# First aggregation of a two-layer graph network: sorted gathers against merged edge blocks scattered with add into four DRAM copies

## The reference

```python
h = relu(layernorm(x))
agg = zeros_like(h).at[src].add(edge_attr)          # first aggregation, key src
...                                                  # attention over one condition row
h = relu(concat([h, agg, x_with_cond], 1) @ W1.T + b1)
x = x + h @ W2.T + b2
h = relu(layernorm(x))
ht = relu(h @ V1 + c1)
msg = sigmoid(exp(wp) * ht[src] + bp)
fsum = segment_sum(msg, dst, 6250)                   # second aggregation, key dst
...                                                  # logit, a matmul, a row norm
```

## Time and profile before

| | us |
|---|---|
| median of three runs | 3203.99 |
| lowest, highest | 3202.18, 3206.39 |
| span of the profiled execution | 4012.8 |
| first aggregation within that span | 368 to 1985 |
| second aggregation within that span | 2201 to 3800 |

### The profile page before, as it was taken

One profiled execution on the slowest core, in us unless ns is written; L12 is line 12 of the kernel. 1 busy time (PEld: TensorE's weight loads), 2 busy tenths in 40 slices (PEclk: granted clock), 3 DMA queues, 4 the chain that ended last, 5 costly groups with the idle time before them and its releaser, 6 DMA issues. The chain is left out here.

```text
span 4012.8 us, 65381 instructions
## 1 busy us (share of the span) xinstructions
PE 2786.4 (69%) x12081; PEld 2045.6 (51%) x12081; DVE 2746.8 (68%) x6119; ACT 2007.6 (50%) x5317; POOL 1848.1 (46%) x1875
## 2 busy tenths in 40 slices
PE   1883777677767776777786677767776777777754
PEld 1552554455545555555575455545555555555543
DVE  7887777667777777677774577777776775444456
ACT  1343565455546554565325455555554655554434
POOL 0225455555554555455312555645555555555400
PEclk9996888888888888888898788888888888888787
DMA  3001222322232223222335222422232223322412
GB/s 105 0 0 46 70 69 71 73 70 69 70 76 68 71 69 79 68 70 65 72 134 169 76 69 72 75 67 69 70 72 74 71 71 69 81 81 81 70 39 77
DMA packets 129255, 287.68 MB, mean 72 GB/s; under 512 B 31200, under 2 KB 59798, under 8 KB 129174
## 3 DMA queue, kind: packets, MB, share of 16 engines
q0 software_dynamic: 84480, 230.80, 22.7%
q1 hardware_dynamic: 42918, 53.84, 4.2%
q10 hardware_dynamic: 1776, 2.23, 0.2%
HBM read 260.68 MB, written 26.06 MB: 71 GB/s over the span
## 5 line engine op out<-in xcount | busy, mean ns | idle before, releaser
L1088 PE MATMUL bank<-oh,ring 128*128 128x256 f32 x7040 | 2110.7, 439 | 351.3 <-DVE agg L888 259.8
L1088 PEld LDWEIGHTS bank<-oh,ring 128*128 128x128 f32 x7040 | 1428.9, 221 | 667.0 <-issue 337.0
L888 DVE TENSOR_TENSOR agg<-bank,agg 128x512 f32 x1760 | 1208.4, 687 | 783.8 <-remote 353.1
L426 POOL DMA_INDIRECT ring<-in_edge_attr,idxst x880 | 877.0, 997 | 766.8 <-DVE idxst L869 501.9
L426 POOL DMA_INDIRECT ring<-g_table,idxst x880 | 850.7, 967 | 735.8 <-DVE idxst L869 457.1
L831 DVE SCALAR_TENSOR_TENSOR ohr<-iota,cst 125x256 f16<-125x256 f16 x1600 | 763.7, 479 | 222.6 <-issue 76.9
L549 ACT ACTIVATE oh<-dist 128x256 f32<-128x256 f32 x1760 | 648.9, 407 | 532.7 <-PE bank L1088 255.9
L536 ACT ACTIVATE dist<-iota,nlst 128x256 f32<-128x256 f32 x1760 | 746.6, 494 | 15.0 <-ACT nlst L530 1.8
L1088 PE MATMUL bank<-mov,ohr 125*128 125x220 f16 x1920 | 379.9, 285 | 457.1 <-DVE mov L639 397.6
L542 ACT ACTIVATE smov<-iota,scst 125x220 f16<-125x220 f16 x560 | 236.7, 469 | 798.8 <-PE bank L1088 422.7
L1088 PEld LDWEIGHTS bank<-mov,ohr 125*128 125x128 f16 x1920 | 170.1, 104 | 654.4 <-DVE mov L639 498.9
(11 more groups left out here) (180 smaller groups left out, 1669.4 us busy)
## 6 DMA issues: line engine op xcount, KB each, us to landing
ring<-in_edge_attr,idxst POOLq DMA_INDIRECT x880
ring<-g_table,idxst POOLq DMA_INDIRECT x880
x_scratch<-ring SPq DMA_DIRECT2D x25, 256.0 KB, 2.0
ring<-x_scratch SPq DMA_DIRECT2D x25, 256.0 KB, 3.4
y_scratch<-ring SPq DMA_DIRECT2D x25, 256.0 KB, 2.4
g_table<-ring SPq DMA_DIRECT2D x25, 256.0 KB, 2.2
pre<-y_scratch SPq DMA_DIRECT2D x25, 256.0 KB, 2.6
agg<-in_x SPq DMA_DIRECT2D x4, 1536.0 KB
```

Of the source, the lines that this page charges most:

```text
L426: gp.indirect_dma_start(out=ring_rows[:, b, j, :], out_offset=None, in_=table, in_offset=bass.IndirectOffsetOnAxis(ap=idxst[:, t:t + 1], a ...
L888: dve.tensor_tensor(to, pt[j][:, :], to, ALU.add).then_inc(s_acc, 1)
L1088: return pe.matmul(o, l, r, start=start, stop=stop, skip_group_check=skip)
```

## The change

The first aggregation has no sort any more (SORTS = 4, all for the second one). The edges are taken in input order.

- SP streams `edge_attr` in 196 blocks of 512 edges (EBLKS, 512 KB each) into four slots that lie in `agg`; partition p holds edges 4p to 4p+3 of the block.
- The keys `src` come once more as floats, transposed by PE in the prologue into `scol`: a column for every tile of 128 edges (ETILES = 784).
- For a tile PE broadcasts the 128 keys along the columns of a PSUM bank (`key_rows`), DVE compares them with the keys on the partitions (`find_same`), masks the result by a triangle and counts it. PE multiplies this 128x128 matrix by the edge rows (`sum_rows`), so that one row of each set of equal keys holds the sum. `first_rows` and `targets` turn the count into an index: the node's row where this is that row, otherwise one of 128 rows behind the nodes ("trash").
- ACT copies the sums from PSUM (two tiles at a time) into eight slots `merged`.
- POOL issues one indirect DMA for each tile, which scatters 128 rows of 1 KB with add into one of four copies of the aggregate in DRAM, tile t into copy t mod 4. Before it POOL waits for the tile that went into the same copy before.
- The four copies, 6400 rows of 1 KB each, are filled with zeros at the start by four DMAs on ACT's queue, behind the weights. Their source is the first tenth of `pre`, so `pre_out` waits for them.
- rank 1 is dealt out over the first 58 blocks, a step a block, on DVE and PE.
- The pass over the windows first adds the copies up: ACT issues four loads of 256 KB for each window into one of two buffers (in `msk` and `cum`), POOL adds them (three adds of 128x512), PE transposes, ACT copies into `agg`; then the pass goes on as before. x is loaded from the end of the front stage on.

The code for the new stage and for this pass is written out without loops.

```diff
-SORTS = 2 * GROUPS
+SORTS = GROUPS
+EB = 4
+EBLK = EB * P
+EBLKS = -(-E // EBLK)
+ETILES = EB * EBLKS
+COPIES = 4
+AROWS = NBLK * P
+ESLOTS = 4
+MSLOTS = 8
+QSLOTS = 3
...
@@ SP
-            sp.wait_ge(s_mm, BODY + GROUPS * TILES)
+            sp.wait_ge(s_h, NW)
+            for b in range(EBLKS):
+                if b >= ESLOTS:
+                    sp.wait_ge(s_m1, 2 * (b - ESLOTS) + 2)
+                rows = P if b + 1 < EBLKS else ELAST
+                sp.dma_start(edge_ring[0:rows, b % ESLOTS, :, :],
+                             a["edge_attr"][b * EBLK:b * EBLK + rows * EB, :].rearrange("(p j) f -> p j f", j=EB)
+                             ).then_inc(s_el[b % ESLOTS], 16)
+
+            sp.wait_ge(s_pv, 2 + NW)
...
@@ POOL
-            gp.wait_ge(s_h, NW)
-            gp.memset(agg[:, :], 0.0).then_inc(s_z, 1)
-            gp.wait_ge(s_a1, 2 + NW)
+            gp.wait_ge(s_zf, 16 * COPIES)
+            for t in range(ETILES):
+                b, j, r = t // EB, t % EB, t % COPIES
+                if j == 0:
+                    gp.wait_ge(s_ix, b + 1)
+                if j % 2 == 0:
+                    gp.wait_ge(s_mg, t // 2 + 1)
+                if t >= COPIES:
+                    gp.wait_ge(s_sa[r], 16 * (t // COPIES))
+                gp.indirect_dma_start(out=aggc_dram[r][:, :], out_offset=bass.IndirectOffsetOnAxis(ap=idx1[:, b, j:j + 1], axis=0),
+                                      in_=merged[:, t // 2 % MSLOTS, (t % 2) * D:(t % 2 + 1) * D], in_offset=None,
+                                      compute_op=ALU.add).then_inc(s_sa[r], 16)
+
+            for n in range(NW):
+                c0, c1, c2, c3 = fold[n % 2]
+                gp.wait_ge(s_fc[n % 2], 16 * COPIES * (n // 2 + 1))
+                gp.tensor_tensor(c0, c0, c1, ALU.add).then_inc(s_fa, 1)
+                gp.tensor_tensor(c2, c2, c3, ALU.add).then_inc(s_fa, 1)
+                gp.wait_ge(s_fa, 3 * n + 2)
+                gp.tensor_tensor(c0, c0, c2, ALU.add).then_inc(s_fa, 1)
...
-            gathers(a["edge_attr"], 0)
...
@@ ACT
+            act.wait_ge(s_zt, 1)
+            for r in range(COPIES):
+                act.dma_start(aggc_dram[r].rearrange("(p c e) f -> p c (e f)", p=P, c=5),
+                              zeros.unsqueeze(1).to_broadcast([P, 5, 10 * D])).then_inc(s_zf, 16)
+
...
                 hold(act, s_a1, n + 3)
+                hold(act, s_zf, 16 * COPIES)
...
-            with act.Fori(0, GROUPS) as g:
-                onehots(g, True)
...
+            for h in range(2 * EBLKS):
+                act.wait_ge(s_m1, h + 1)
+                if h >= MSLOTS:
+                    for t in (2 * (h - MSLOTS), 2 * (h - MSLOTS) + 1):
+                        act.wait_ge(s_sa[t % COPIES], 16 * (t // COPIES + 1))
+                act.copy(merged[:, h % MSLOTS, :], pt[h % 4][:, :]).then_inc(s_mg, 1)
...
+            def fold_load(n):
+                if n >= 2:
+                    act.wait_ge(s_ft, n - 1)
+                for r in range(COPIES):
+                    act.dma_start(fold[n % 2][r].rearrange("p (j f) -> p j f", j=2), copies[r][n]).then_inc(s_fc[n % 2], 16)
...
+            for n in range(NW):
+                if n + 2 < NW:
+                    fold_out(n + 2)
+                if n + 4 < NW:
+                    fold_load(n + 4)
+                act.wait_ge(s_t1, n + 3)
+                act.activation(slot2k(ring, CHB + n % CHB), pre[:, n * CH:(n + 1) * CH], ACT.Relu).then_inc(s_r, 1)
...
@@ DVE
-            rank(1, Chain(dve, s_sort, links))
-            dve.wait_ge(s_z, 1)
+            second = Chain(dve, s_sort, links)
+            dve.wait_ge(s_h, NW)
+
+            def find_same(b):
+                dve.wait_ge(s_sr, b + 1)
+                if b >= QSLOTS:
+                    dve.wait_ge(s_m1, 2 * (b - QSLOTS) + 2)
+                for j in range(EB):
+                    r = dve.scalar_tensor_tensor(out=same[:, b % QSLOTS, j, :], in0=(pA, pB)[b % 2][:, j * P:(j + 1) * P],
+                                                 scalar=scol[:, (b % 2) * EB + j, b // 2:b // 2 + 1], in1=low[:, :],
+                                                 op0=ALU.is_equal, op1=ALU.mult, accum_out=seen[:, b, j:j + 1])
+                r.then_inc(s_same, 1)
...
+            for b in range(EBLKS + 1):
+                if b < EBLKS:
+                    find_same(b)
+                if 0 <= b - 1 < EBLKS:
+                    first_rows(b - 1)
+                if b < RANK_STEPS:
+                    rank_step(1, second, b)
+                if 0 <= b - 1 < EBLKS:
+                    targets(b - 1)
...
-            with dve.Fori(0, GROUPS) as g:
-                group_with_sort(g, True)
...
@@ PE
+            def key_rows(b):
+                if b >= 2:
+                    pe.wait_ge(s_same, b - 1)
+                for j in range(EB):
+                    key = scol[:, (b % 2) * EB + j, b // 2:b // 2 + 1].to_broadcast([P, P])
+                    r = mm((pA, pB)[b % 2][:, j * P:(j + 1) * P], key, ident[:, :], True, True)
+                r.then_inc(s_sr, 1)
...
+                    r = mm(pt[h % 4][:, (j % 2) * D:(j % 2 + 1) * D], same[0:rows, b % QSLOTS, j, :],
+                           edge_ring[0:rows, b % ESLOTS, j, :], True, True)
```

More of the change, by code:

```diff
@@ L566, in _, with fold_out @@
             act.wait_ge(s_a1, 2 + NW)
-            with act.Fori(0, GROUPS) as g:
-                onehots(g, True)
-            with act.Fori(0, CBODIES) as i:
-                for q in range(CHB):
-                    n = i * CHB + q
-                    hold(act, s_t1, n + 3)
-                    act.activation(slot2k(ring, CHB + q), pre[:, bass.ds(n * CH, CH)], ACT.Relu).then_inc(s_r, 1)
+            for h in range(2 * EBLKS):
[4 more added lines that the diff above has]
+                act.copy(merged[:, h % MSLOTS, :], pt[h % 4][:, :]).then_inc(s_mg, 1)
+            copies = [t.rearrange("(c j p) f -> c p j f", p=P, j=2) for t in aggc_dram]
+            def fold_load(n):
[3 more added lines that the diff above has]
+                    act.dma_start(fold[n % 2][r].rearrange("p (j f) -> p j f", j=2), copies[r][n]).then_inc(s_fc[n % 2], 16)
+            def fold_out(n):
+                act.wait_ge(s_ft, n + 1)
+                act.copy(agg[:, n * CH:(n + 1) * CH], (pA, pB)[n % 2][:, :]).then_inc(s_fe, 1)
+            for r in range(COPIES):
+                act.wait_ge(s_sa[r], 16 * ETILES // COPIES)
+            act.wait_ge(s_rank, 2)
+            fold_load(0)
+            fold_load(1)
+            fold_out(0)
+            fold_load(2)
+            fold_out(1)
+            fold_load(3)
+            for n in range(NW):
[5 more added lines that the diff above has]
+                act.activation(slot2k(ring, CHB + n % CHB), pre[:, n * CH:(n + 1) * CH], ACT.Relu).then_inc(s_r, 1)
             act.wait_ge(s_var, 2)
@@ L607, in _ @@
             act.wait_ge(s_t3, 2 + NW)
[L608 removed]
+            with act.Fori(0, SORTS - 1) as g:
                 onehots(g, True)
@@ new lines, in _, with fold_transpose @@
+            key_rows(0)
+            for b in range(EBLKS):
+                if b + 1 < EBLKS:
+                    key_rows(b + 1)
+                sum_rows(b)
+                if b < RANK_STEPS:
+                    rank_step(1, b)
+            def fold_transpose(n):
+                pe.wait_ge(s_fa, 3 * n + 3)
+                if n >= 2:
+                    pe.wait_ge(s_fe, n - 1)
+                for j in range(2):
+                    for k in range(KD):
+                        r = pe.transpose((pA, pB)[n % 2][:, k * WIN + j * P:k * WIN + (j + 1) * P],
+                                         fold[n % 2][0][:, j * D + k * P:j * D + (k + 1) * P], ident[:, :])
+                r.then_inc(s_ft, 1)
@@ new lines, in sums_product @@
+            def sums_product(n):
+                pe.wait_ge(s_fe, n + 1)
+                pe.wait_ge(s_t1, n + 1 + (n % CHB == 0))
+                for m in range(KD):
+                    for k in range(KD):
+                        r = mm(pt[n % CHB % 2][:, m * WIN:(m + 1) * WIN], wT(w1bT, k, m),
+                               agg[:, n * CH + k * WIN:n * CH + (k + 1) * WIN], k == 0, k == 1)
+                r.then_inc(s_p1, 1)
+            fold_transpose(0)
+            fold_transpose(1)
+            sums_product(0)
```

151 lines of the change are left out of this document (100 added, 51 removed).

## The result

| | before | after |
|---|---|---|
| median of runs, us | 3203.59 | 3539.82 |
| lowest, highest, us | 3202.18, 3206.39 | 3535.08, 3540.51 |
| span of the profiled execution, us | 4012.8 | 3533.4 |

The ratio is 1.105, with an interval of 1.1035 to 1.1067: the change makes the kernel 336 us slower. The forecast was 3100 us, 440 us too low, and of the wrong sign; the time also lies above the range (3460 us).

What follows compares the result with a forecast made beforehand. DVE and POOL were taken as both near their limit. To the end of the pass, 1661 us becomes 356 + 1058 + 12 + 130 = 1556 us; 3204 - 105 = 3099, say 3100 us, range 2990 to 3460 us.

Steps and rivals of the forecast that it cites:

- The 1.37 us a tile: Both aggregations of the kernel before, 880 tiles each: 2407 us of the 3204 us median, 1203 us for the first.
- the crawls: Small DVE register steps of 0.70 us instead of 0.06 and 0.31 us in the before profile, read as recording cost.
- The pace p: POOL's time per scatter in the first aggregation: 1.35 us taken, 784 tiles making 1058 us instead of 1203.
- rival 1: Scatter costs POOL more than the gather: 3453 us at 1.8 us a tile, 3766 us at 2.20; chance 0.24.
- The removed work, PE, DVE, ACT, edge loads: First aggregation loses sorts, one-hots and DVE add; PE, DVE, ACT and edge loads each stay below 1.25 us a tile.
- Flight and copies: A scatter into DRAM takes 5 us to land; with four copies a quarter, 1.25 us, bounds the tile pace.
- Front stage: Time before the first scatter: 320 + 30 + 3 + 3 = 356 us instead of 368.
- the term of the zeroing: Zeroing 26.2 MB at the start delays x by 0 to 91 us; 30 us taken, with equal shares.
- Fold: Adding up the copies in the pass over windows: 5.2 us a chunk, 130 us against 90 before, plus 12 us draining.
- The third: Ends cost more: zeroing delays x by the full 91 us (+61), fold takes 240 us (+110): 3271 us; chance 0.06.
- The second: Four copies are too few: flight 6.35 us, 1.59 us a tile in the first aggregation, 3288 us; chance 0.16.
- the fourth: Everything hides: 1.25 us a tile in the first aggregation and no delay of x, 2992 us; chance 0.10.

Runs made afterwards that it cites:

- The first batch: Earliest follow-up runs, several variants of the changed kernel; the kernel before, run unchanged beside them, had a median of 4077 us.

## Why the prediction was wrong, step by step

**What bounds before.** The 1.37 us a tile held up: the second aggregation in the record without crawls takes 1170 us, 1.33 us a tile, and the first would be 1.40 us by the estimate above. The explanation did not: I took the crawls for the cost of recording. The first batch had plain runs just as slow (4077 us), and the later profiles had no crawls, with the same kernel (the scatters without add) at 1619 and at 1170 us in its second aggregation. So the recording does not bring them on; what does stays open. Since the sum was made against the median, the mistaken cause cost only the 0.04 us a tile between 1.37 and 1.33, which made the error 34 us smaller.

**The pace p: the step that failed.** I took 1.35 us between 1.25 and 2.20 us; it is 1.857 us, and 784 x 0.51 = 397 us of the 440 are here. The choice followed the gather's rows because the scatter was "the same instruction", and the add was given nothing. The run without the add had 1.315 us: as an estimate of a plain scatter 1.35 us was good, but the priced thing was another one. The bounds did hold the value, and the middle that I used for rival 1 (1.8 us) was nearly it. Rival 1 was the right mechanism with the right place; it deserved more than 0.24, since the only statement on the add that I had spoke for it and nothing measured spoke against it. By the Trainium skill, "Collectives: The Full Stack", Part 3, a reduce emits two read descriptors where a copy emits one. The estimate that the prediction drew from it, twice the gather's 0.95 us, was 1.90 us for the instruction, and 1.55 us was measured. The runs show what goes by the row doubled, from 1.0 to 2.0 ns, but that is 0.13 of 0.97 us, and a fixed 0.45 us comes on top.

**The removed work, PE, DVE, ACT, edge loads.** Right: the compare takes 348 ns (0.35 taken), the copy 586 ns, and together they would allow 0.65 us a tile. A bottleneck set by POOL makes their savings worth nothing.

**Flight and copies.** Right in the mean: 5 us taken, 4.85 us measured, and 9 us of waits in the whole stage. That the waits are so few is owed to the slow pace: at the forecast's pace they would have come, as the plain scatters show with their 76.7 us, 0.10 us a tile.

**Front stage.** 356 us forecast, 391 us measured. Without any zeroing in the way it is 318.9 us (326 forecast), so the term of the zeroing is 72 us and not 30, near the top of its bounds (91). Two things made it so. "Equal shares" holds by packets, not by bytes, as the rows of the two queues show: x's 1 KB packets against the zeroing's 10 KB packets give x a tenth. And 97 rows made the keys' load a single file, beside which x came only from about 60 us on, which no step had.

**Fold.** 5.2 us a window forecast, 6.0 us measured; with the drain 164 us instead of 142. The adds and their number were right (3.8 us). The mis-sized term is issue and landing of a window's loads: 5.4 us were taken (at 289 GB/s), 1937.44 - 1930.04 = 7.4 us measured, while the stage moved 227 GB/s.

**The table pass** was costed at no change and takes 12 us more; why was not examined.

The sum of these steps: +35 (front) + 398 (scatters) + 22 (drain and fold) + 12 (table pass) - 34 (second aggregation) + 1 (end) = +434 of the 440 us. Of the rivals, the first came in. The third came in by a third: 57 us of its 171. The second did not at this pace, nor did the fourth, whose 1.25 us even the plain scatters missed by 0.07 us.

## What to carry to other kernels

A DMA that adds is not the DMA that copies: measure its issue on POOL (here 1.55 us against 0.97 us for 128 rows) before a plan rests on one of them for each tile. Its cost is nearly fixed for each instruction, so fewer rows win little back and narrower rows nothing; that fewer instructions would was not tried. When a change trades balanced work on four engines for one instruction on one engine, that one instruction's price times its count is the forecast; price the thing itself or give the rival that prices it otherwise half of the chance. Bulk traffic that is "off the path" (zeroing) goes behind the small loads that the path needs.

## What the runs showed of the hardware

- An indirect DMA of 128 rows of 1 KB holds POOL for 0.97 us, whether it gathers or scatters, and for 1.55 us when it adds; 64 rows take 0.905 and 1.42 us; 128 rows of 512 B with add take 1.55 us. 0.30 us lie between two of them wherever nothing else holds POOL up.
- In the packet records of these stretches a plain scatter of 128 KB leaves 32 packets of 4 KB (169 ns each on average), the adding one 128 packets of 1 KB (129 ns each). So the same bytes take 16.5 us of the DMA engines' time instead of 5.4 us for each tile: the scatters' queue has a share of 0.57 in the changed kernel (400 to 1840 us) and 0.26 without the add (400 to 1420 us), though there it moves the same bytes in less time.

```profile
q0 software_dynamic: 111832, 101.84, 57.0%
```

```profile
q0 software_dynamic: 37317, 101.95, 26.4%
```

- A flight of an adding scatter, from start to the landing that releases the next into the same copy, is 4.85 us on average with two copies (3.95 to 7.12 us where the next one waited), and three in flight lose 0.08 us a tile at a pace of 1.86 us.
- Two queues share the DMA engines packet by packet: 10 KB packets beside 1 KB packets leave the latter a tenth of the time. A load of 97 partitions went in single file, one of 96 did not.
